# First attention of a four-stage transformer block: masked quarters of the diagonal blocks left out of scores and products, units put in another order

## The reference

```python
q = jnp.einsum('bnd,fd->bnf', x, Wq).reshape(b, n, H, DH).transpose(0, 2, 1, 3)
k = jnp.einsum('bnd,fd->bnf', x, Wk).reshape(b, n, H, DH).transpose(0, 2, 1, 3)
v = jnp.einsum('bnd,fd->bnf', x, Wv).reshape(b, n, H, DH).transpose(0, 2, 1, 3)
sim = jnp.einsum('bhid,bhjd->bhij', q, k) * SCALE
sim = SOFTCLAMP * jnp.tanh(sim / SOFTCLAMP)
causal = jnp.tril(jnp.ones((n, n), dtype=bool))
sim = jnp.where(causal, sim, jnp.finfo(sim.dtype).min)
attn = jax.nn.softmax(sim, axis=-1)
out = jnp.einsum('bhij,bhjd->bhid', attn, v)
out = out.transpose(0, 2, 1, 3).reshape(b, n, H * DH)
return jnp.einsum('bnf,df->bnd', out, Wo)
```

## Time and profile before

| what | value |
|---|---|
| median of 3 runs | 1210.4 us (1209.5 to 1213.53) |
| the profiled execution | 1209.32 us |
| its span, first to last instruction | 1207.6 us |
| mean granted TensorE clock | 0.969 of full |
| TensorE busy in the whole span | 1123.9 us (93%) |
| first attention in the trace | about 56 to 416 us |
| TensorE busy from 150 to 200 us | 49.6 of 50 us |
| VectorE, ScalarE, GpSimd in the same 50 us | 38.7, 38.5, 32.4 us |
| scores L841, products L860 | 151.8 and 171.9 us busy |
| exp and tanh L511, L516 | 146.3 and 143.7 us busy |
| masks L488 | 54.2 us busy |

### The profile page before, as it was taken

The page is one execution under the profiler, slowest core; times in us unless marked ns, Lnnn a source line. Parts: engine busy times, 40 slices in busy tenths (PEclk is TensorE's granted clock), DMA queues, the critical chain, the costliest instruction groups (busy, mean ns, idle before and its releaser), DMA issues. The chain is left out here.

```text
span 1207.6 us, 29026 instructions
## 1 busy us (share of the span) xinstructions
PE 1123.9 (93%) x10965; PEld 626.1 (52%) x10965; DVE 860.9 (71%) x1805; ACT 705.3 (58%) x915; POOL 522.8 (43%) x529
## 2 busy tenths in 40 slices
PE   3799999999999998879997999999999999888998
PEld 1456566566565684468983322222222222547996
DVE  6466878778778565864425899999999992585441
ACT  4687877877777435512215177777777778441220
POOL 0066667567666400348852114323421331026883
PEclk9999999999999997879999999999999999697999
DMA  4000010010010101327752212222222210414765
GB/s 129 1 9 24 23 42 25 18 42 24 18 42 20 39 19 57 122 75 190 183 114 60 75 34 69 61 56 58 61 61 55 59 47 18 143 49 115 182 166 123
DMA packets 61625, 81.82 MB, mean 68 GB/s; under 512 B 24768, under 2 KB 42564, under 8 KB 60892
## 3 DMA queue, kind: packets, MB, share of 16 engines
q1 hardware_dynamic: 49420, 70.54, 19.2%
q0 software_dynamic: 10880, 8.86, 5.0%
q10 hardware_dynamic: 1232, 1.19, 0.3%
HBM read 55.12 MB, written 15.72 MB: 59 GB/s over the span
## 5 line engine op out<-in xcount | busy, mean ns | idle before, releaser
L2015 ACT ACTIVATE at_PR<-psum 128x1024 f32<-128x1024 f32 x256 | 248.0, 1021 | 98.8 <-PE psum L2256 96.8
L2084 DVE TENSOR_REDUCE at_MX<-psum 128x1 f32<-128x512 f32 x468 | 298.3, 684 | 6.3 <-PE psum L2233 3.6
L511 ACT ACTIVATE PR<-psum 128x1024 f32<-128x1024 f32 x144 | 146.3, 1021 | 72.2 <-PE psum L841 61.4
L860 PE MATMUL psum<-PR,V 64*64 64x256 f32 (+1 forms) x2560 | 171.9, 357 | 4.0 <-issue 1.5
L841 PE MATMUL psum<-Q,K 64*64 64x512 f32 (+2 forms) x1792 | 151.8, 437 | 2.1 <-ACT PR L511 2.1
L860 PEld LDWEIGHTS psum<-PR,V 64*64 64x64 f32 x2560 | 96.3, 133 | 98.9 <-issue 88.8
L516 ACT ACTIVATE PR<-PR 128x1024 f32<-128x1024 f32 x144 | 143.7, 1050 | 0.0
L2273 PE MATMUL psum<-at_PR,at_VG 128*32 128x512 f32 x1024 | 136.2, 604 | 0.8 <-POOL at_PR L1952 0.8
L1549 PE MATMUL psum<-moe_XGT,moe_WE 128*128 128x256 f32 x512 | 124.5, 388 | 0.6 <-ACT moe_XGT L1237 0.6
L1952 POOL TENSOR_TENSOR at_PR<-at_PR,at_FAC 128x512 f32<-128x512 f32 x64 | 81.1, 1268 | 97.1 <-ACT at_PR L2015 97.1
L488 POOL TENSOR_SCALAR_AFFINE_SELECT PR<-PR 128x256 f32<-128x256 f32 (+1 forms) x80 | 54.2, 682 | 155.4 <-ACT PR L516 155.1
(11 more groups left out here) (265 smaller groups left out, 1855.0 us busy)
## 6 DMA issues: line engine op xcount, KB each, us to landing
moe_WE<-in_c_We SPq DMA_DIRECT2D x32, 768.0 KB
XB<-at_r_dram SPq DMA_DIRECT2D x32, 256.0 KB, 3.8
at_outs_dram<-at_OTS SPq DMA_DIRECT2D x15, 256.0 KB, 3.0
moe_rows_dram<-XNS SPq DMA_DIRECT2D x2, 1152.0 KB, 11.6
moe_spare_dram<-moe_zeros SPq DMA_DIRECT2D x2, 1024.0 KB, 14.0
moe_sum_dram<-XB SPq DMA_DIRECT2D x2, 1024.0 KB, 3.8
moe_SG<-moe_spare_dram SPq DMA_DIRECT2D x8, 256.0 KB
at_KU<-in_c_max_krows SPq DMA_DIRECT2D x16, 128.0 KB
```

What stands on the lines that cost most here:

```text
L511: act.activation(PR[u][:, :, :], S[(b + u) % 2][:, :, :], ACT.Tanh, scale=SCALE0 / CLAMP).then_inc(z.clamped, 1)
L860: mm = pe.matmul(O[row[h], q:q + w], V[rows, b, j, row[h]], PR[u][rows, h, at:at + w], start=(first and u == 0), stop=(not first and u == ...
L2015: act.activation(PR[:, gu % PRS, 2 * r:2 * r + 2, :].rearrange("p h n -> p (h n)"), g.psum[:, 2 * r * BANK:(2 * r + 2) * BANK], ACT.Exp).t ...
L2084: dve.tensor_reduce(MX[:, c // 32 % 2, 8 * (c % 2) + 4 * pair + I % 4, khalf:khalf + 1], bank(("max", c))[:, :], AX, ALU.max).then_inc(z.r ...
```

## The change

The quarter of each diagonal block that is masked altogether is no longer computed: `hidden` gives the 64 columns that scores and products leave out where the key half is the later one. For four of the eight key blocks (`SWAPPED`) the two key halves change places in the tiles (`half`, `keys`), in K and in V alike. In each unit with diagonal blocks one side is turned and one is not, and the scores take their pieces in turn from both sides, so a short piece stands beside a long one on the two column halves. The diagonal blocks, which were in the first, fourth, sixth, seventh and ninth unit, are now in the third, the fourth and the sixth, which has four. Masks are two operations per such unit: a selection for blocks that are not turned, and a multiplication by a fixed triangle TRI (made at the start) for the turned ones. `ADDS` follows the new units. `READ_LAST` says how far the additions of the pass before must be before ScalarE overwrites a tile. The value projection stays on 64 x 64 tiles and takes its tokens by `keys`.

```diff
-DIAGS = [[n * P for n, (j, i) in enumerate(u) if j == i] for u in BLOCKS]
-ADDS = [[(256, slice(2, 3), (0, slice(1, 2)), None)],
-        [],
...
+BLOCKS = [[(0, 2), (0, 3), (0, 6), (0, 7)], [(1, 2), (1, 3), (1, 6), (1, 7)], [(2, 2), (2, 3), (0, 0), (0, 1)],
+          [(4, 4), (4, 5), (6, 6), (6, 7)], [(2, 4), (2, 5), (2, 6), (2, 7)], [(3, 3), (5, 5), (1, 1), (7, 7)],
+          [(3, 4), (3, 5), (3, 6), (3, 7)], [(0, 4), (0, 5), (4, 6), (4, 7)], [(1, 4), (1, 5), (5, 6), (5, 7)]]
+SWAPPED = (0, 1, 6, 7)
...
+ADDS = [[],
+        [(256, slice(0, 4, 3), (0, slice(0, 2)), (1, slice(0, 2)))],
...
+        def half(j, c):
+
+            return 1 - c if j in SWAPPED else c
+
+        def keys(j, c):
+
+            return j * P + DH0 * half(j, c)
+
+        def hidden(j, q, c):
+
+            return DH0 if half(j, c) == 1 and q == ORDER.index(j) * P else 0
...
-            if u == 0:
+            if u == 1:
                 wait(eng, z.totalled, s - 1)
...
+                    plain, turned = (v[:, 0::2, :], v[:, 1::2, :]) if u == ALL_DIAGONAL else (v[:, 0::4, :], v[:, 2::4, :])
+                    count = plain.shape[1]
+                    pool.affine_select(out=plain, in_=plain, compare_op=ALU.is_ge, fill=0.0, base=0,
+                                       pattern=[[0, count], [1, P]], channel_multiplier=-1).then_inc(z.masked, 1)
+                    pool.tensor_tensor(turned, turned, bcast(TRI[:, :].unsqueeze(1), [P, count, P]), ALU.mult
+                                       ).then_inc(z.masked, 1)
...
-                    through = ADDED[max(u, 4) + 1] - ADDED[NU]
+                    through = ADDED[READ_LAST[u] + 1] - ADDED[NU]
...
-                    for j, at, q, w in (near if joined else near + far):
+                    for j, at, q, w in (near if joined else [piece for pieces in zip(near, far) for piece in pieces]):
                         for h in range(2):
                             for c in range(2):
-                                into, of = S[(b + u) % 2][row[c], h, at:at + w], Q[row[h], b, q:q + w]
+                                skip = hidden(j, q, c)
+                                into, of = S[(b + u) % 2][row[c], h, at + skip:at + w], Q[row[h], b, q + skip:q + w]
...
                             for j, at, q, w in PIECES[u][side][n:n + 1]:
+                                skip = hidden(j, q, part)
                                 for h in range(2):
-                                    mm = pe.matmul(O[row[h], q:q + w], V[rows, b, j, row[h]], PR[u][rows, h, at:at + w],
+                                    mm = pe.matmul(O[row[h], q + skip:q + w], V[row[part], b, j, row[h]],
+                                                   PR[u][row[part], h, at + skip:at + w],
```

More of the change, by code:

```diff
@@ L310 @@
         [(256, slice(1, 4, 2), None, (8, slice(0, 2)))]]
+READ_LAST = [1, 1, 2, 4, 4, 5, 6, 7, 8]
 ADDED = [sum(len(a) for a in ADDS[:u]) for u in range(NU + 1)]
-MASKED = [sum(1 for d in DIAGS[:u] if d) for u in range(NU + 1)]
+MASKED = [MASKS * sum(DIAGS[:u]) for u in range(NU + 1)]
 ROWS = 32
@@ L340, in stage_front @@
         "totalled copied spread inverted kept broad scaled wo summed added passed "
-        "halved part_projected").split())
+        "halved part_projected triangle").split())
     with ExitStack() as tmp:
@@ L500, in _ @@
                 pool.memset(g.ones[:, :], 1.0).then_inc(z.ones, 1)
+                pool.memset(TRI[:, :], 1.0).then_inc(z.triangle, 1)
+                pool.wait_ge(z.triangle, 1)
+                pool.affine_select(out=TRI[row[0], :], in_=TRI[row[0], :], compare_op=ALU.is_ge, fill=0.0, base=-DH0,
+                                   pattern=[[1, P]], channel_multiplier=-1).then_inc(z.triangle, 1)
+                pool.wait_ge(z.triangle, 2)
+                pool.affine_select(out=TRI[row[1], 0:DH0], in_=TRI[row[1], 0:DH0], compare_op=ALU.is_ge, fill=0.0, base=0,
+                                   pattern=[[1, DH0]], channel_multiplier=-1).then_inc(z.triangle, 1)
+                pool.wait_ge(z.triangle, 3)
                 span(pair)(pool)
@@ L788, in project_first @@
                             for c in range(2):
-                                first = k % 2 * BANK + t * P + DH0 * c
+                                first = keys(4 * (k % 2) + t, c)
                                 mm = pe.matmul(J[k % 2][row[c], t * P:(t + 1) * P], g.XT[:, first:first + DH0],
@@ L840, in scores @@
                                     of = split(Q[row[h], b, :], 2 * P)[:, q // (2 * P)::(far[0][2] - q) // (2 * P), :]
-                                mm = pe.matmul(into, K[row[h], b, j * P + DH0 * c:j * P + DH0 * (c + 1)], of,
+                                mm = pe.matmul(into, K[row[h], b, keys(j, c):keys(j, c) + DH0], of,
                                                start=True, stop=True, skip_group_check=True)
@@ L856, in multiply @@
                         for side in range(2):
-                            rows = row[side if first != swap else 1 - side]
+                            part = side if first != swap else 1 - side
                             for j, at, q, w in PIECES[u][side][n:n + 1]:
+                                skip = hidden(j, q, part)
                                 for h in range(2):
-                                    mm = pe.matmul(O[row[h], q:q + w], V[rows, b, j, row[h]], PR[u][rows, h, at:at + w],
+                                    mm = pe.matmul(O[row[h], q + skip:q + w], V[row[part], b, j, row[h]],
+                                                   PR[u][row[part], h, at + skip:at + w],
                                                    start=(first and u == 0), stop=(not first and u == NU - 1),
```

28 lines of the change are left out of this document (13 added, 15 removed).

## The result

The changed kernel takes 1223.7 us (median of six runs, 1218.4 to 1227.4), the kernel before, run beside it, 1212.0 (1209.5 to 1214.5): a ratio of 1.010, interval 1.007 to 1.013. It is slower by 1%. The forecast was 1207.3 with a range of 1198.5 to 1214. The profiled execution took 1227.4 us for a span of 1225.7, so 18.1 us of the difference have to be found in the trace.

What follows compares the result with a forecast made beforehand. TensorE's own work was taken to bound the first attention: 13.7 us saved, less debits of 0.2, 0.7, 0.2 and 1.0, is 11.6; less 8.5 at boundaries, 3.1 net. Forecast 1207.3 us beside the median 1210.4, range 1198.5 to 1214.

Steps and rivals of the forecast that it cites:

- the first debit: Scores of third and fourth unit: two pieces each instead of one cost TensorE 0.2 us in all.
- TensorE's saving: Shortened scores and products save TensorE 0.43 us each per pass, 0.86 together, 13.7 us over 16 passes.
- rival C: Rounds last as long as their widest matmul, so scores save nothing: slower by 1.8 us, 1212.2; chance 0.15.
- The boundaries: Between passes, VectorE's copies of O wait behind a later addition and delay TensorE's products: 8.5 us over 15 boundaries.
- Into an odd pass: Boundary where the copies of O begin at 172.15 instead of 171.60: 0.55 us later each, seven times.
- Into an even pass: Boundary where VectorE is the slow one: copies late by 0.4 to 0.7 us, taken as 0.55, seven times.
- At the first boundary: Copies of O begin at 83.80 instead of 82.97: 0.8 us lost, once.
- rival D: VectorE bounds the second half of odd passes, TensorE waits at the totals: 1215.3 with 1.2 us of delay; chance 0.15.
- its small debits: Debits on TensorE's matmuls: 0.2 us in all for two-piece scores, 0.7 us for matmuls of 64 columns.
- The last pass: TensorE's wait for GpSimd's mask of the sixth unit grows by 1.0 us (0.5 to 1.5).
- The net: Whole kernel: 11.6 us saved before the boundaries, less 8.5 at them, 3.1 us faster.

Runs made afterwards that it cites:

- b_unroll: The kernel before with TensorE's loop written out, the other engines as they are: 1208.2 us, ratio 0.9963 to the kernel before.
- a_pad64: The changed kernel with 64 semaphore increments at the very start of TensorE's queue: 1203.9 us, ratio 0.9953 to the kernel before.
- a_v128_p250: The changed kernel with the value projection on 128 rows and 250 increments at the start of TensorE's queue: 1236.6 us.
- a_pad56: The changed kernel with 56 semaphore increments at the start of TensorE's queue: 1254.9 us in one run.
- b_split2: The kernel before with the second and fifth unit's scores in two pieces each, eight more matmuls per pass: 1225.9 us, ratio 1.0085.
- b_pad106: The kernel before with 106 semaphore increments at the start of TensorE's queue: 1229.6 us in one run.
- b_pad150: The kernel before with 150 semaphore increments at the start of TensorE's queue: 1235.5 us, ratio 1.0263.

## Why the prediction was wrong, step by step

**The step that failed is the first debit.** "The third and fourth unit now need two pieces each in the scores, units before had one. Between nothing and 0.01 us each; I take 0.2 us in all." As work on the array that is right (0.76 us against the ideal 0.75). But a piece is also instructions. The recorded instructions of a turn grow from 1626 to 1686, and in the program the loop moves from 1845 to 3471 to 1941 to 3627: the passes written out ahead of it have grown by 96. By the rule of the table above the body alone would still have fitted (1845 + 1686 = 3531); body and shift together carry its end over a border. The term of 0.2 us measures 19.4 us (325.97 - 306.53), in two ways: TensorE stands still at the turn and once more, for 1.1 us, later in it, and in two of the three refetched turns it works at the lower clock for 3.4 and 6.8 us. With that term in its place the profiled time follows: 1209.3 - 3.1 + 19.4 = 1225.6, and 1227.4 was measured.

Nor did any rival hold this. They asked which engine waits for which; that TensorE could wait for its own program was in none, though the view of queues had a row for it. The kernel before executes some 23000 instructions on TensorE, 90 blocks of 256 (b_unroll has 88 packets), and fetched 58. That the loop was held, and that this could end, was there to be read.

The Trainium skill ("Runtime: NRT & Kernel Launch", "Instruction fetch mechanics") gives TensorE a buffer of 2048 instructions, filled in blocks of 16 KiB or 256 instructions. The trace agrees with the 16 KB (1.41 MB in 86 packets), and a hold of seven but not eight blocks is what such a buffer would give if one block of it is taken by fetching ahead; no run shows that last part. It also says that a taken branch forces a fetch when its target is outside "the current 2-page window". By that, the kernel before would fetch at each of its turns, and it has no packet from 148 to 373 us: here the measurement decides, against the two pages.

**TensorE's saving** (0.86 us per pass) was right; in a_pad64 these steps are 0.83 us shorter per pass. Products of 192 columns take 0.32 or 0.33 us, scores 0.76 and 0.67, the two narrow rounds of the sixth unit 0.23 (forecast 0.22 to 0.26). So rival C falls: rounds of unequal widths do not last as long as their widest. With it falls, for these tiles, the rule of the Trainium skill ("TensorE: Matmul & The Clock Gate", "Part 3: Packing small matmuls — row/col tiling") that matmuls start and end strictly in program order: by it the scores would have taken 0.86 us, and the measured 0.76 decides.

**The boundaries** were right in mechanism, and a little smaller. Into an odd pass 0.32 us are lost (1.47 against 1.15) where 0.55 was forecast. Into an even pass it is 0.21 (1.38 against 1.17), also against 0.55. At the first boundary 0.84 are lost (1.70 against 0.86), against 0.8. But in every odd pass the totals now wait for VectorE's copy of V, in a_pad64 here:

```profile
190.18 0.64 PE L890 MATMUL psum<-PR,V 64*64 64x256 f32 x8
...
191.04 1.07 PE L904 MATMUL psum<-XN,ones 128*32 128x512 f32 x8 [0.22 <-DVE V L671]
```

0.86 us between these rows. Before, the row ahead of the totals at 188.95 was this one, 0.56 us sooner:

```profile
188.39 0.63 PE L860 MATMUL psum<-PR,V 64*64 64x256 f32 x8
```

This is the mechanism of rival D, at 0.30 us and not at the 1 that it needed. Together a pair of passes saves 1.66 and gives back 0.83 at these three places. Another 0.17 goes in four steps at the value projections, each 0.02 to 0.07 us longer than before. That leaves 0.66; 0.65 was measured (43.79 us against 44.44). The forecast made it 0.51 (1.72, less 0.11 for its small debits and 1.1 for two boundaries).

**The last pass.** Forecast was a wait about 1.0 us longer for the sixth unit's mask. From the products ahead to those behind the mask it is 2.37 us in the changed kernel, against 1.71 before (402.92 to 404.63), so 0.66 more, and 0.88 more in a_pad64: within the forecast's 0.5 to 1.5. The selection alone took 1.63 us there, beside an addition of VectorE, where 0.75 had been put in; over the whole stage such selections average 0.70. The boundary into the last pass, which the forecast had as one of its seven at 0.55, is longer than the others. There TensorE already stood idle before the change:

```profile
394.70 0.66 PE L860 MATMUL psum<-PR,V 64*64 64x256 f32 x8 [1.46 <-issue]
```

From the products ahead of it to this row it is 2.07 us, and 2.70 after the change: 0.63 more.

**The net** without the refetch: the forecast said 3.1 us faster. The stage became 3.8 us shorter in the loop (a_pad64) and 1.3 when written out, with the stop of 1.8 us in it. Of the medians, a_pad64 is 0.5% (6 us; by the interval 3 to 9) under the kernel before. Without the refetch the change is worth about what was forecast.

## What to carry to other kernels

When a change adds instructions inside an engine's loop, or ahead of it, count them, not only their time, and look at the queue of instruction packets in the profile of before: clearly fewer packets than blocks of 256 executed instructions means a loop that is being held, and a place from which it may stop being held. In the profile after, idle time put down to "issue" at the first instruction of a turn, with the other engines idle as well, is its mark; increments at the start of that engine's queue, where it waits anyway, leave the loop as it is and tell this from everything else. Try more than one count: 64 cured this kernel and 56 made it worse. And an instruction that waits for something late should not stand ahead of one for which the busiest engine waits.

## What the runs showed of the hardware

- TensorE's loop of six turns was fetched in the first and held over the other five in the six kernels where it touched seven blocks of 256 instructions (but for one packet at 260 us in a_v128_p250), and refetched in the five where it touched eight (or where it started in the last 80 instructions of a block, which these runs can't tell apart). In a_pad56 it was refetched in every turn, in the other four in every second one: in the second, fourth and sixth turn of the changed kernel, in the third and fifth of b_split2, b_pad106 and b_pad150. What sets this rhythm is open; in a_pad56 the first border lies only five to eight instructions behind the loop's start.
- A refetch cost a turn 5.4 to 10.1 us (a pass of 27.2 to 31.5 us instead of 22): 2.9 to 6.5 us idle at the turn, and behind 12 of the 14 the granted clock at its lower level for 3.4 or 6.8 us.
- 141 increments of a semaphore at the start of a queue delayed it to 22.6 us, some 0.15 us each; 66 in a turn of the loop cost 0.6 us, 0.009 each, under the matmuls.
- Four 64x64 tiles went on independently where their widths differ (256 and 192 columns in 0.76 us, 128 and 64 in 0.67). A value projection on 128x64 tiles between rows on 64x64 tiles cost about 0.3 us more than one on 64x64 tiles (1.03 against 0.89, and 0.46 against 0.37 and 0.48 against 0.44 beside it).
